# Writing an attention and FFN program out without its loops, and copying the score mask into PSUM on ScalarE

## What is computed

```python
h = _layernorm(x) * (1 + ca) + sa
x = x + ga * attention(h)                       # full attention, 1024 keys
h = _layernorm(x) * (1 + cb) + sb
for i in range(6):                              # DEPTH
    q, k, v = heads(shift_tokens(h) @ Wqkv[i])  # 16 heads of 64
    q, k = rotary(l2norm(q) * qs), rotary(l2norm(k) * ks)
    mask = (it < jb) | (it > jb + 32) | (jb == -1)
    sim = where(mask, -max, einsum(q, k) * 8)   # 32 queries by 64 keys per window
    h = softmax(sim) @ v @ Wo[i] + h
    y = shift_tokens(h)
    a, gate = split(layernorm(y) @ W1[i] + b1[i])
    h = (a * gelu(gate)) @ W2[i] + b2[i] + h
x = x + gb * h
```

## Time and profile before

| | |
|---|---|
| median of three runs | 3659.52 us (3654.99 to 3666.93) |
| profiled execution | 3657.72 us, its span 3655.9 us |
| TensorE busy | 3440.4 us (94%) |
| VectorE busy | 2639.6 us (72%) |
| ScalarE busy | 2510.0 us (69%) |
| POOL busy | 2356.1 us (64%) |
| granted TensorE clock, mean | 0.97 |

### The profile page before, as it was taken

The page is one execution under the profiler, slowest core; times in us unless marked ns, Lnnn a source line. Parts: engine busy times, 40 slices in busy tenths (PEclk is TensorE's granted clock), DMA queues, the critical chain, the costliest instruction groups (busy, mean ns, idle before and its releaser), DMA issues.

```text
span 3655.9 us, 132252 instructions
## 1 busy us (share of the span) xinstructions
PE 3440.4 (94%) x50548; PEld 2655.9 (73%) x50548; DVE 2639.6 (72%) x5823; ACT 2510.0 (69%) x5117; POOL 2356.1 (64%) x1568
## 2 busy tenths in 40 slices
PE   7979999999999999999999999999999999999997
PEld 5658777777777777777777777777777777777774
DVE  5668777778777778777677777777767677777773
ACT  3447777777666777766677776677767677766773
POOL 2048677677666677666676766677766667666661
PEclk9989999999999999999999999999999999999998
DMA  2001111211111211111111111111111121111111
GB/s 80 2 14 49 34 44 41 62 41 50 36 42 37 62 37 51 40 35 43 58 41 37 50 41 35 50 54 38 52 35 39 36 65 40 47 40 39 41 37 44
DMA packets 98219, 157.34 MB, mean 43 GB/s; under 512 B 18128, under 2 KB 39632, under 8 KB 96720
## 3 DMA queue, kind: packets, MB, share of 16 engines
q1 hardware_dynamic: 93440, 132.73, 13.4%
q10 hardware_dynamic: 4176, 15.74, 1.3%
HBM read 20.48 MB, written 2.10 MB: 6 GB/s over the span
## 4 chain that ended last, share of the span: by engine, by line
PE 78%; issue 7%; ACT 5%; POOL 1%; DVE 1%; ACTq 0%; DMA 0%; DVEq 0%; POOLq 0%; SPq 0%
PE psum L797 20%; PE psum L821 12%; PE psum L887 9%; PE psum L907 7%; PE psum L844 6%; PE psum L864 4%; PE psum L852 4%; PE psum L927 4%; PE psum L939 3%; PE psum L932 3%; PE psum L816 2%; PE psum L918 1%; PE psum L914 1%; ACT probT L592 1%; ACT qbd L585 1%
## 5 line engine op out<-in xcount | busy, mean ns | idle before, releaser
L388 POOL TENSOR_TENSOR qkr<-qks,rnorm 128x1024 f32<-128x1024 f32 x384 | 731.3, 1905 | 388.0 <-issue 291.4
L380 POOL TENSOR_TENSOR qks<-work 128x1024 f32<-128x1024 f32 x384 | 908.0, 2365 | 72.2 <-DVE work L1148 67.9
L396 POOL TENSOR_TENSOR probn<-prob,psumr 128x512 f32<-128x512 f32 x384 | 400.6, 1043 | 542.9 <-DVE psumr L1174 542.9
L575 ACT ACTIVATE sq<-psum 128x512 f32<-128x512 f32 x768 | 463.9, 604 | 366.9 <-PE psum L797 366.2
L797 PE MATMUL psum<-whi,xhi 128*128 128x512 f32 x1152 | 571.8, 496 | 113.0 <-issue 79.1
L1122 DVE TENSOR_REDUCE ssq<-sq 128x8 f32<-128x512 f32 x768 | 516.6, 680 | 54.4 <-ACT sq L575 18.6
L1146 DVE TENSOR_TENSOR work<-psum,rot 128x512 f32<-128x512 f32 x768 | 508.3, 662 | 51.1 <-POOL qks L380 41.9
L1180 DVE TENSOR_REDUCE nmax<-psum 128x8 f32<-128x512 f32 x384 | 265.1, 690 | 380.7 <-PE psum L821 379.4
L821 PEld LDWEIGHTS psum<-kT,qbd 128*64 128x64 f32 x12288 | 411.6, 143 | 127.0 <-issue 126.8
L821 PE MATMUL psum<-kT,qbd 128*64 128x64 f32 x12288 | 468.5, 231 | 13.3 <-issue 13.2
L797 PE MATMUL psum<-whi,xlo 128*128 128x512 f32 x1152 | 464.5, 403 | 0.0
(11 more groups left out here) (131 smaller groups left out, 6488.8 us busy)
## 6 DMA issues: line engine op xcount, KB each, us to landing
vsh<-vtok SPq DMA_DIRECT2D x384, 192.0 KB, 2.4
vsh<-vtok SPq DMA_DIRECT2D x384, 64.0 KB, 3.0
xsh<-xs_in SPq DMA_DIRECT2D x192, 64.0 KB, 2.4
ff_x<-x_mid SPq DMA_DIRECT2D x96, 128.0 KB
wqkv<-Wqkv_dram ACTq DMA_DIRECT2D x5, 1536.0 KB, 6.7
wo_next<-Wo_dram ACTq DMA_DIRECT2D x5, 512.0 KB, 8.2
xtok<-x_dram SPq DMA_DIRECT2D x4, 512.0 KB, 11.0
out_dram<-qkr SPq DMA_DIRECT2D x8, 256.0 KB, 2.5
```

The source lines that it names most:

```text
L380: pool.tensor_tensor(qks[:, :, :], rcos, rsin, ALU.add).then_inc(s["add_ready"], 1)
L388: pool.tensor_tensor(qkr[:, j % 2, :, :], qks[:, :, :], rnorm[:, :].unsqueeze(2).to_broadcast([P, 2 * OCT, DH]), ALU.mult).then_inc(s["qkr ...
L396: pool.tensor_tensor(probn[:, :, :], prob[:, j % 2, :, :], psumr[:, j % 2, 1, :].unsqueeze(2).to_broadcast([P, OCT, KEYS]), ALU.mult).then ...
L575: act.activation(sq[:, w * OCT:(w + 1) * OCT, :], bank[w].rearrange("p (h n) -> p h n", n=DH), ACT.Square).then_inc(s[("sqq_ready", "sqk_r ...
```

## The change

The loops go. Each engine's program is a plain Python loop over 400 steps whose waits have constant values; `Turn`, `sweep`, `wait_apart`, `wait_all` and the register counts disappear. The order of the work in a step is kept on each engine. Some waits are added on TensorE: for `pts_ready` before the FFN's matmuls into bank 4 and for `x_mid_ready` before the output product. The final loops that write the result are written out too.

The mask matmul goes. ScalarE copies the mask into bank 3 (`mask_seeded`), at the start of its step, ahead of `x_high` and `k_turned`; it waits for `sub_ready` of the unit before and signals `seed_ready`. The score matmuls wait for `seed_ready` and all have `start=False`. One mask matmul with `start=True` stands before the first step (`bits_set`), so that the later ones add to what lies in the bank. Cut to its core:

```diff
-        def need(eng, what, base, off, first=False):
-            if first and off <= 0:
-                return
-            eng.wait_ge(s[what], base + off)
...
-        def sweep(eng, body):
...
-            turn(0, 0, first=True, ffn=False)
-            turn(0, 1, ffn=False)
-            with eng.Fori(2, ITERS - 1) as it:
-                turn(0, it)
-            with eng.Fori(0, DEPTH - 1) as layer:
-                turn(layer, ITERS - 1, renew=True)
-                turn(layer + 1, 0, renew=True)
-                turn(layer + 1, 1, renew=True)
-                with eng.Fori(2, ITERS - 1) as it:
-                    turn(layer + 1, it)
-            turn(DEPTH - 1, ITERS - 1)
-            turn(DEPTH, 0, last=True)
-            turn(DEPTH, 1, last=True, drained=True)
+        def need(eng, what, value):
+            if value > 0:
+                eng.wait_ge(s[what], value)
...
+            def mask_seeded(n):
+                if not is_unit(n):
+                    return
+                if n == 0:
+                    act.wait_ge(s["bits_set"], 1)
+                need(act, "sub_ready", n)
+                entry = 1 if n // UPT % TPB else 0
+                act.activation(bank[3].rearrange("p (a k) -> p a k", a=PAIRS),
+                               mask[:, entry:entry + 1, :, :].rearrange("p a b k -> p a (b k)").to_broadcast([P, PAIRS, 2 * KEYS]),
+                               ACT.Copy).then_inc(s["seed_ready"], 1)
...
+            for step in range(STEPS + 2 * UNROLL):
+                weights_fetched(renewed_at(step, -8))
+                output_renewed(renewed_at(step, 6))
+                high_renewed(renewed_at(step, -1), 0, 1)
+                high_renewed(renewed_at(step, 0), 2, 3)
+                high_renewed(renewed_at(step, 2), 4)
+                high_renewed(renewed_at(step, 3), 5)
+                ffn_renewed(renewed_at(step, 15))
+                ffn_square(block_at(step, 2))
+                mask_seeded(step - 3)
+                x_high(step)
+                k_turned(step - 3)
+                exponential(step - 4)
+                ffn_affine(block_at(step, 4))
+                ffn_inverse(block_at(step, 3))
+                attended(step - 6)
+                ffn_gates(block_at(step, 4))
+                square(step, 0)
+                inverse_norm(step - 1)
+                q_turned(step - 2)
+                probabilities_turned(step - 5)
+                values(step - 3)
+                square(step, 1)
...
-                        need(pe, "qk_ready", units, j + 1)
-                        need(pe, "sub_ready", units, j, first)
-                        entry = 1 if ti or j < 0 else (it % 2 if isinstance(it, int) else pe.snap(it % 2))
-                        m = mask[:, bass.ds(entry, 1), :, :].rearrange("p a b k -> p a (b k)").to_broadcast([P, PAIRS, 2 * KEYS])
-                        pe.matmul(bank[3].rearrange("p (a k) -> p a k", a=PAIRS), ident_bf[:, :], m,
-                                  start=True, stop=False, skip_group_check=True)
...
+                need(pe, "qk_ready", n + 1)
+                need(pe, "seed_ready", n + 1)
+                for a in range(PAIRS):
+                    for w in range(4):
+                        c = (a * 2 + w // 2) * KEYS
+                        mm = pe.matmul(bank[3][w % 2 * 64:w % 2 * 64 + 64, c:c + KEYS],
...
+                                       start=False, stop=(a == PAIRS - 1 and w >= 2), skip_group_check=True)
+                mm.then_inc(s["sim_ready"], 1)
...
+                need(pe, "x_mid_ready", tile)
...
+                need(pe, "pts_ready", min(b * UNROLL + 2 * UNROLL - 5 + 1, STEPS))
...
+            pe.matmul(bank[3].rearrange("p (a k) -> p a k", a=PAIRS), ident_bf[:, :],
+                      mask[:, 0:1, :, :].rearrange("p a b k -> p a (b k)").to_broadcast([P, PAIRS, 2 * KEYS]),
+                      start=True, stop=True, skip_group_check=True).then_inc(s["bits_set"], 1)
+            for step in range(STEPS + 2 * UNROLL):
+                ffn_up(block_at(step, 4))
+                projection(step, 0)
+                ffn_down(block_at(step, 5))
+                scores(step - 3)
```

More of the change, by code:

```diff
@@ L10 @@
 from contextlib import ExitStack
-from dataclasses import dataclass
 import concourse.bass as bass
@@ L57, with block_at, renewed_at, is_unit @@
 NORM_AT = {bw: n for n, bw in enumerate(NORMS)}
[L60 to L79, removed]
+def block_at(step, place):
+    b = step // UNROLL - 2
+    return b if step % UNROLL == place and 0 <= b < DEPTH * BLOCKS else None
+def renewed_at(step, place):
+    layer = (step - place) // UNITS
+    return layer if (step - place) % UNITS == 0 and 0 < layer < DEPTH else None
+def is_unit(n):
+    return 0 <= n < STEPS
 def build(nc, x, w_attn, b_qk, b_v, Wqkv, Wo, W1, W2, cols, b1_cols, gains, c_t, wmod, rot_tab, out):
@@ L264, in body @@
[L264 to L299, removed]
@@ new lines, in exponential, with ffn_square @@
+            def exponential(n):
+                if not is_unit(n):
+                    return
+                need(act, "sub_ready", n + 1)
+                need(act, "pn_ready", n - 1)
+                act.activation(prob[:, n % 2, :, :], sdiff[:, :, :], ACT.Exp).then_inc(s["p_ready"], 1)
+            def ffn_square(b):
+                if b is None:
+                    return
+                act.wait_ge(s["f_xc"], b + 1)
+                act.activation(ff_n[:, :], ff_x[:, :], ACT.Square).then_inc(s["f_sq"], 1)
@@ L693, in _ @@
         @block.tensor
         def _(pe):
-            counts_of[pe.engine] = [pe.alloc_register(f"pe_count{k}") for k in range(4)]
             pe.wait_ge(s["silu_ready"], 1)
@@ new lines, in turn_probabilities @@
+            def turn_probabilities(n, *ffn_in_4):
+                if not is_unit(n):
+                    return
+                need(pe, "pn_ready", n + 1)
+                need(pe, "pts_ready", n)
+                for b, what, value in ffn_in_4:
+                    if b is not None:
+                        pe.wait_ge(s[what], value(b))
+                for a in range(PAIRS):
+                    mm = pe.transpose(bank[4][:, a * P:(a + 1) * P], probn[:, 2 * a:2 * a + 2, :].rearrange("p h n -> p (h n)"), ident[:, :])
+                mm.then_inc(s["pt_ready"], 1)
@@ new lines, in output @@
+            def output(n):
+                if not is_unit(n) or n % UPT == 0:
+                    return
+                tp, tile = n // UPT % 2, n // UPT
+                need(pe, "aot_ready", n + 1)
+                need(pe, "vs_ready", min(n + 4, STEPS))
+                need(pe, "x_mid_ready", tile)
+                if tile % TILES == 0:
+                    pe.wait_ge(s["wo_moved"] if tile else s["wo_in"], tile // TILES if tile else 16)
+                for k in range(HEADS // 2):
+                    mm = pe.matmul(bank[5][:, 0:P], wo[:, k, :], aoT[:, tp, k, :],
+                                   start=(k == 0), stop=(k == HEADS // 2 - 1))
+                mm.then_inc(s["wo_ready"], 1)
@@ new lines, in ffn_down @@
+            def ffn_down(b):
+                if b is None:
+                    return
+                pe.wait_ge(s["w2_in"], b // BLOCKS * 16 + 16)
+                pe.wait_ge(s["f_u"], b * CH + CH)
+                need(pe, "pts_ready", min((b + 2) * UNROLL, STEPS))
+                for ch in range(CH):
+                    mm = pe.matmul(bank[4], w2[0:CW[ch], ch, :], gel[0:CW[ch], ch, :], start=(ch == 0), stop=(ch == CH - 1))
+                mm.then_inc(s["f_y"], 1)
+            pe.wait_ge(s["mask_ready"], 10)
@@ L966, in _ @@
+            for i in range(BLOCKS // 2):
                 for h in range(2):
@@ L977, in _ @@
         def _(dve):
-            counts_of[dve.engine] = [dve.alloc_register(f"dve_count{k}") for k in range(2)]
             norms_done = [0]
```

906 lines of the change are left out of this document (415 added, 491 removed).

## The result

| | before | after |
|---|---|---|
| median | 3662.82 us (3654.99 to 3666.93, 4 runs) | 3430.64 us (3428.06 to 3432.49, 4 runs) |
| profiled execution, its span | 3657.72, 3655.9 us | 3432.49, 3430.7 us |
| TensorE busy | 3440.4 us (94%) | 3290.3 us (96%) |
| ScalarE busy | 2510.0 us (69%) | 2683.1 us (78%) |
| mean granted clock of TensorE | 0.970 | 0.987 |

The ratio is 0.937, with a 95% interval of 0.935 to 0.939: 232 us off. The forecast was 3428 us. The total is right to 3 us; two of its terms are not, and they cancel. The experiments separate them.

What follows compares the result with a forecast made beforehand. TensorE, busy 94% of the span, was taken to bound the kernel. 3657.7 us less 164 (loops) less 123 (masks) plus 56 (copies) gave 3426.7, forecast as 3428 us for the median; range 3380 to 3515 us.

Steps and rivals of the forecast that it cites:

- Part 1: TensorE's 28 loop edges: writing the loops out saves 164 us, 5.8 us an edge from stall and slow stretch behind.
- The renewals extra: The three turns per layer that renew the weights cost 6.05 us extra per layer, loops or no loops.
- The reading of the transfers: Instruction fetch: 7.86 MB for 132252 executed instructions, 59 bytes each, so straight code adds no fetching.
- Rival 3: TensorE's instruction stream: straight code fetched end to end doesn't keep up, so slower, 3764 us at 0.7 us a packet; chance 0.04.
- rival 2: Loop edges: the stall isn't the branch's and stays in straight code; only the mask's 67 us remain, 3593 us; chance 0.10.
- Part 2: Mask matmul leaves TensorE: 0.32 us for each of 384 masks, 123 us off.
- The low bound: Mask matmul on TensorE worth only 0.23 us, the spacing of the matmuls before it: 88 us in all.
- Part 3: Mask copies on ScalarE give back 56 us: 1.0 us in each of 48 FFN turns, 1.5 us per layer in renewals.
- step 5: Step of a turn where ScalarE waits for the group norms: the mask's gain partly melts, 0.2 us.
- Rival 1: ScalarE becomes the bound; copy costs as much as the mask matmul, only the loops pay: 3495 us; chance 0.22.
- Rival 4: All mask copies on ScalarE are hidden, nothing given back: 3373 us; chance 0.07.
- What would show it: Signs on TensorE: no issue idle over 1 us before projections, clock 1.00, turns 64 to 65 us, aoT waits 0.6 to 0.9.

Runs made afterwards that it cites:

- loop_pe: Kernel before with the loops of all engines but TensorE written out, TensorE's kept: 3660.14 us, ratio 0.999.
- straight_pe: Kernel before with the loops written out in TensorE's program alone, the other four engines still looping: 3505.33 us, ratio 0.956.
- straight_all: Kernel before with the loops written out for all engines, the mask matmul kept: 3480.85 us, ratio 0.950.
- no_seed: Changed kernel with the mask copied by ScalarE only once, before the first unit, so the scores come out different: 3401.85 us, ratio 0.929 to before.
- seed_twice: Changed kernel with a second copy of the same shape, into a spare tile, ahead of each mask copy: 3483.39 us, ratio 0.952 to before.
- seed_after_gates: Changed kernel with the mask copy in the FFN's step moved behind the Gelu instructions, the other seven of eight staying: 3405.87 us, ratio 0.930 to before.
- seed_in_loops: Kernel before with its loops kept, ScalarE copying the mask into PSUM in place of TensorE's mask matmul: 3551.93 us, ratio 0.970.

## Why the prediction was right, point by point

**TensorE bounds the kernel, and an edit is worth what it takes off its sequence: right.** loop_pe and straight_pe show it directly. Four engines lost their loops and the time stayed; TensorE lost them and it fell by 155 us.

**Part 1, the loops, 164 us: right in mechanism, 16 us too small.** Measured alone they are worth 180 us (3660.5 to 3480.9), 6.4 us an edge. The term that was mis-sized is the straight turn. I took the one sample of 66.17 us from 641.80 to 707.97, in which the other engines still loop; with all written out it is 65.97 us. That is 43 x 0.20 = 9 us. The prediction had costed the register waits at nothing by the distance from mask to scores alone; the 0.2 us stand at line 887. The renewals extra are 5.4 us a layer and not 6.05, 3 us in all. Outside the 43 turns lie the 3 us that were forecast. The other 4 of the 16 us are the difference between the profiled execution of before and the median beside straight_all, and the rounding. The method, a difference against straight code and not a sum of stalls, was the right one: the row of stalls has 79.1 us, fewer than half of the 180, and even the whole idle time of TensorE has only 109 us of them.

The reading of the transfers was wrong in its number, though not in its conclusion. I divided 7.86 MB by all instructions. Queue 8 is TensorE's alone, and the straight program fetches 1.1 MB less there, not the same; on queue 14 it fetches 0.5 MB more (1.01 MB before, 1.54 MB in straight_all). Rival 3, straight code starving TensorE, did not happen: straight_all shows one wait for "issue" before the projections, 3.5 us ahead of the first unit, which before has too.

The rule by which a branch costs 0.05 to 0.1 us (the Trainium skill, page "Advanced Engine Details and Errata", section "Control Flow Timing") and rival 2 that hung on it are refuted: every stall at the 28 edges went with TensorE's loops. The figure may hold for the branch itself, which no run here separates; the 6.4 us are the fetch, as the packets at the stalls show, and the slow stretch behind it.

**Part 2, 0.32 us a mask, 123 us: wrong, it is 0.22 to 0.23 us, 84 to 88 us in all.** The low bound was the true value. Before, the scores began 0.55 us behind the last projection matmul; after, they begin 0.33 us behind it. I had forecast 0.23, by taking the whole distance between the mask matmul and the first score as the mask's. But the scores start 0.32 us behind the mask matmul and 0.33 us behind the projection: nearly the same distance behind either. TensorE's busy time fell by 3373.8 - 3290.3 = 83.5 us from straight_all to after, which is 383 x 0.22. The prediction named this possibility ("the rest may belong to the start of the scores and stay") and then chose the other end.

**Part 3, 56 us given back: right in the place, too large in size.** The wait for aoT grew by 0.73 us a turn to 0.88 us, inside the forecast of 0.6 to 0.9 us. Of the 0.73, 0.23 is the mask's own gain in that step, lost as the prediction said, and 0.5 the copy: no_seed confirms the 0.52. The 0.2 us that I put on step 5 do not exist: 65.97 - 8 x 0.23 + 0.73 = 64.86 us, the turn of after, leaves nothing for it (with 0.22 us a mask the sum is 64.94). The renewals: five layers of after take 33.6 us more than 43 x 64.86, those of straight_all 27.3 us more than 43 x 65.97, so the copies cost 1.3 us a layer where I had 1.5. In all 48 x 0.73 + 6 = 41 us given back, against 56. no_seed agrees: without the copies the time is 29 us shorter, and the mask's own gain that is lost in the FFN's step is 48 x 0.23 = 11 us.

The mask's net worth so is 88 - 41 = 47 us by these terms, and 3480.85 - 3430.64 = 50 us by measurement, against the 67 us forecast. No run takes the mask alone out of straight_all, so the 50 us also hold whatever the register loads cost that straight_all still has (its page counts 4740 instructions more than that of after). The sum: 16 us too little for the loops and 17 us too much for the mask. The forecast hit because two errors had opposite signs, and not because its terms were that good; the range, 3380 to 3515, was about right for what I knew.

**The rivals.** Rival 1 (ScalarE becomes the bound, and a copy costs the 0.32 us that the mask matmul did) fell by no_seed and seed_twice: the 384 copies cost 29 us, 0.08 us each, and 384 further ones 0.14 us each. ScalarE's busy time grew by 173 us and not by 230, since the copies overlap their neighbours: `x_high`'s start follows 0.52 us behind a copy that lasts 0.62 us, as the timeline of ScalarE in after shows:

```profile
1476.67 0.62 ACT L543 ACTIVATE psum<-mask 128x512 f32<-128x512 bf16 x1
1477.19 0.43 ACT L491 ACTIVATE xhi<-xsh 128x256 fp32r<-128x256 f32 x1
```

The Trainium skill, page "ScalarE: Activation LUTs", section "What ACT_TABLE_LOAD costs", gives 186 ns + 0.833 ns per element for an activation with immediate scale and bias, and an overlap of 93 ns. An estimate from it is 186 + 0.833 x 512 = 613 ns, and 0.52 us of sequence; the rows agree. Rival 4 (all copies hidden) was nearer: seven in eight are, and it needs only the move of seed_after_gates to make it eight. Its 3373 us was still too low, for the same 0.32 us.

**What would show it.** No "issue" idle before the projections: seen. A granted clock of 1.00: seen, in the turn from 429.52 on (stretch; its length; busy us of PE, PEld, DVE, ACT, POOL; clock, DMA, GB/s) as in the earlier trace rows, while TensorE is busy 63.98 us of it. Of the 46 stretches from one first FFN matmul to the next, 41 have it in after and 19 before.

```profile
429.52:494.38 64.86, 63.98 (x1023) 50.43 (x1023) 52.01 (x115) 53.76 (x112) 47.82 (x32) 1.00 0.17 43
```

Turns 64 to 65 us apart: seen. Scores 0.23 us behind the projection: not seen, 0.33.

## What to carry to other kernels

Write out the loops of the engine that bounds the kernel, and of that one first; the loops of the others cost nothing measurable before that and 24 us (0.7%) after it. The matmul that left TensorE's busy sequence was worth its own spacing there (0.23 us), not the whole distance to the start of what followed it (0.32 us): the scores keep their distance to whatever now stands ahead. When work moves to an engine with room, only the places where that engine is itself the chain cost anything: find them, and put the new work behind them.

## What the runs showed that was not expected

**A loop edge has no fixed price.** Sixty-four satisfied waits outside all loops cost 41 us, 128 of them gained 52 us. A comparison of two looped kernels can move by over 1% on that alone, as seed_in_loops did. The packets of TensorE's instruction queue beyond those of straight code (46 to 70 here) tell the two groups apart, and the packets in the stretch of one stall (one, two or three) tell how long it is.

**The stall is only part of the price, and the clock goes with the rest.** From straight_all to before TensorE's idle time grows by 109 us and its busy time, for the same matmuls, by 67 us. In before and seed_in_loops what an inner edge costs beyond its stalls has three sizes: 0.4 to 0.7 us where the granted clock of the turn is 1.00, 1.8 to 2.2 us where it is 0.98, and 3.1 to 3.6 us where it is 0.95, as TensorE falls to the 1.2 GHz level for a longer part of it. In before the three shortest stalls (1.68 to 2.16 us) left the clock at 1.00, and the other 21 inner edges did not. But the length alone does not decide it. In seed_in_loops two stalls of 2.01 us ended at 2179.2 and at 2247.0 us; behind the first TensorE stayed at the 2.4 GHz level, behind the second it fell (columns as in the earlier trace rows):

```profile
2179.20:2184.20 5.00, 4.98 (x58) 3.98 (x62) 2.88 (x6) 3.22 (x8) 3.12 (x2) 1.00 0.02 3
2247.00:2252.00 5.00, 5.00 (x46) 4.04 (x47) 1.58 (x3) 1.78 (x5) 3.05 (x2) 0.66 0.01 3
```

With its shorter stalls seed_in_loops kept the clock at 9 of 24 inner edges, before at 3. So its edges gained in the stalls and behind them. That the clock is the cause of the further loss is read from the windows' granted clock; no run separated it from the fetch.
